# Keeping the FFN's transposed input in DRAM between the two halves of an attention and FFN kernel

## The reference, cut to what matters

```
xn  = layernorm(x, eps=1e-5)
attention:
  xm  = xn * time_mix + shift_by_one_token(xn) * (1 - time_mix)
  k   = exp(min(xm @ Wk.T, 60));  v = xm @ Wv.T;  r = xm @ Wr.T
  wkv, sum_k = decayed sums over earlier tokens of k * v and of k (16 heads, T = 1024)
  a   = (sigmoid(r) * wkv / (sum_k + 1e-16)) @ Wo.T
ffn:
  xf    = layernorm(xn, eps=1e-3) * ln_gamma + ln_beta
  gamma = max |xf| over ALL tokens and channels;  beta = mean |weight|
  w_q   = clip(round(weight / (beta + 1e-5)), -1, 1)
  xq    = clip(xf * 128 / gamma, -128 + 1e-5, 128 - 1e-5)
  f     = (xq @ w_q) * (gamma * beta / 128)
out = x + a + f
```

## Time and profile before

| | |
|---|---|
| runs | 988.46, 988.88, 989.01 us; median 988.88 |
| profiled execution | span 987.2 us, first to last instruction; its own time is not given apart from the span |
| instructions | 14552 |
| DMA | 72.81 MB, 36520 packets on SP's queue, 20.9% of 16 engines |
| chain that ended last | PE 41%, DVE 28%, issue 14%, ACT 10%, DMA 4%, POOL 2% |

### The profile page before, as it was taken

How to read it: one execution, slowest core, us unless ns; L and a number is a source line. 1 busy time by engine, 2 the same in 40 slices (tenths; PEclk the granted TensorE clock), 3 DMA queues, 4 the chain that set the end, 5 groups by cost and what they waited for, 6 DMA issues and landing times.

```text
span 987.2 us, 14552 instructions
## 1 busy us (share of the span) xinstructions
PE 936.3 (95%) x4418; PEld 757.4 (77%) x4418; DVE 806.9 (82%) x1418; ACT 549.3 (56%) x881; POOL 278.9 (28%) x428
## 2 busy tenths in 40 slices
PE   5589999999999999997999999999999999999998
PEld 4478778777877787775787877887878778788786
DVE  5788988889888989895788787797888787878875
ACT  5365756666665757474554454646555546556432
POOL 4332424152415232432303314024023050230300
PEclk9889999999999999999999999999999999999999
DMA  8010302030302121213104113131131221320302
GB/s 317 24 43 25 104 31 97 0 127 0 111 17 86 41 85 42 85 42 128 37 34 144 43 44 129 42 128 63 64 129 42 85 85 42 106 72 36 129 1 85
DMA packets 36560, 72.81 MB, mean 74 GB/s; under 512 B 1180, under 2 KB 1192, under 8 KB 36520
## 3 DMA queue, kind: packets, MB, share of 16 engines
q1 hardware_dynamic: 36520, 72.36, 20.9%
HBM read 47.19 MB, written 25.17 MB: 73 GB/s over the span
## 4 chain that ended last, share of the span: by engine, by line
PE 41%; DVE 28%; issue 14%; ACT 10%; DMA 4%; POOL 2%; DVEq 0%; ACTq 0%; SPq 0%; POOLq 0%
PE kvr L403 7%; PE kvr L405 7%; PE kvr L404 7%; DVE scans L802 7%; PE out_banks L436 5%; PE out_banks L438 5%; PE transposed L342 4%; DVE bn_stats L677 3%; PE out_banks L418 3%; PE out_banks L420 2%; PE out_banks L419 2%; DVE rwkv_lo L822 2%; DVE k_and_kv L792 2%; DVE k_and_kv L818 2%; DVE evacuated L725 2%
## 5 line engine op out<-in xcount | busy, mean ns | idle before, releaser
L968 POOL TENSOR_SCALAR normed<-x,own_stats 128x512 f32<-128x512 f32 x68 | 88.7, 1312 | 239.2 <-PE transposed L342 231.9
L948 POOL TENSOR_SCALAR stat_work<-mean_var 128x4 f32<-128x4 f32 x32 | 10.9, 339 | 344.8 <-DVE mean_var L682 319.8
L403 PE MATMUL kvr<-xm_hi,wv_hi 128*128 128x512 f32 x256 | 107.4, 419 | 0.0
L403 PE MATMUL kvr<-xm_hi,wk_hi 128*128 128x512 f32 x256 | 106.5, 416 | 0.0
L403 PE MATMUL kvr<-xm_hi,wr_hi 128*128 128x512 f32 x256 | 105.8, 413 | 0.0
L418 PE MATMUL out_banks<-wo_hi,rwkv_hi 128*128 128x512 f32 x256 | 103.0, 402 | 2.4 <-DVE rwkv_lo L822 2.4
L405 PE MATMUL kvr<-xm_hi,wv_lo 128*128 128x512 f32 x256 | 101.7, 397 | 0.0
L420 PE MATMUL out_banks<-wo_hi,rwkv_lo 128*128 128x512 f32 x256 | 101.2, 395 | 0.0
L419 PE MATMUL out_banks<-wo_lo,rwkv_hi 128*128 128x512 f32 x256 | 101.2, 395 | 0.0
L436 PE MATMUL out_banks<-w_ternary,ffn_hi 128*128 128x512 f32 x256 | 100.4, 392 | 0.7 <-DVE ffn_lo L749 0.5
L404 PE MATMUL kvr<-xm_lo,wv_hi 128*128 128x512 f32 x256 | 100.9, 394 | 0.0
(11 more groups left out here) (126 smaller groups left out, 2151.3 us busy)
## 6 DMA issues: line engine op xcount, KB each, us to landing
x<-in_L_attn_x SPq DMA_DIRECT2D x16, 1024.0 KB, 5.3
other<-in_L_attn_x SPq DMA_DIRECT2D x16, 1024.0 KB, 5.3
attn_scratch<-x SPq DMA_DIRECT2D x8, 1024.0 KB, 4.3
parked<-attn_scratch SPq DMA_DIRECT2D x8, 1024.0 KB, 6.7
out<-parked SPq DMA_DIRECT2D x8, 1024.0 KB, 4.3
out<-x SPq DMA_DIRECT2D x7, 1024.0 KB, 4.4
parked<-in_L_attn_Wk SPq DMA_DIRECT2D x1, 1024.0 KB, 7.9
other<-in_L_attn_Wv SPq DMA_DIRECT2D x1, 1024.0 KB, 10.1
```

What stands on the lines that cost most here:

```text
L403: nc.tensor.matmul(KVR[:, m, :], hi, XH[t][:, ch, :], start=(ch == 0), stop=False)
L968: last = G.tensor_scalar(dst[:, q, :], src[:, q, :], stats[:, 2 * ffn, q:q + 1], stats[:, 2 * ffn + 1, q:q + 1], ALU.mult, ALU.add)
```

## The change

- Half A stores each FFN slot as it is evacuated (gamma and beta applied, before any scaling) to a DRAM tensor `ffn_input`, 256 KB a slot, 16 slots a batch, from `U`, which becomes a ring of four. ACT waits for the store of a buffer before it writes it again.
- Half B has no FFN transposes, no statistics and no normalisation of "other", and none of own tiles for the FFN. SP loads each chunk into ZA, once ACT has read the chunk of the tile before; ACT copies it from ZA into `U`, scaled by 128 / gamma in the same instruction. Clip, split, low part and ffn_out stay as they are. PE's slots of kinds ffn_* are left out.
- At the seam, the first tile of B is loaded from DRAM within the last batch of A. The reduction of the maximum and POOL's all-reduce are moved into that batch (DVE at group 21), the four scalar operations before the adds of attn1, and the ternary weights are made in four pieces in groups 13 to 16. `gamma_scaled` and `beta_scaled` are gone.
- SP's program is written out batch by batch, with the stores and loads between its old issues.

The diff, cut to its core:

```
-        U = sb("evacuated", [P, 2, TILE])
+        U = sb("evacuated", [P, RING, TILE])
...
-        RING = 2
+RING = 4
...
+    ffn_in = nc.dram_tensor("ffn_input", (B, 2, CH, P, TILE), F32, kind="Internal").ap()
...
+            def store_ffn_input(b, n):
+                kind, ch = SLOTS[n]
+                bb = b + HALF if "other" in kind else b
+                sp.wait_ge(act_u, slots_before(b, "A", n) + 1)
+                sp.dma_start(ffn_in[bb, int(kind[-1]), ch], U[:, n % RING, :]).then_inc(s_fst[n % RING], 16)
+
+            def batch_a(b, is_last=False):
+                for n in range(7):
+                    store_ffn_input(b, n)
+                sp.wait_ge(pe_t, slots_before(b, "A", first_slot("ffn_other0") + CH))
+                sp.dma_start(ZA[:, :, :], x_t[b + HALF, 1]).then_inc(s_oth, 16)
+                store_ffn_input(b, 7)
+                store_ffn_input(b, 12)
+                sp.wait_ge(dve_out, BANKS + bank_use(b, "A", "attn0") + Q)
+                sp.dma_start(scratch_t[b, 0], X[0][:, :, :]).then_inc(s_xst[0], 16)
+                store_ffn_input(b, 13)
+                sp.wait_ge(s_xst[0], 16 * b + 16)
+                sp.dma_start(X[0][:, :, :], x_t[b + 1, 0]).then_inc(s_x[0], 16)
+                for n in range(14, 19):
+                    store_ffn_input(b, n)
...
+                if is_last:
+                    for r in range(RING):
+                        sp.wait_ge(s_fst[r], 16 * CH * HALF)
+                    sp.wait_ge(pe_t, slots_before(b, "A", first_slot("ffn_other1") + CH))
+                    for ch in range(CH):
+                        sp.dma_start(ZA[:, ch, :], ffn_in[HALF, 0, ch]).then_inc(s_fld[ch], 16)
...
+            def load_ffn_input(b, what, ch):
+                bb = b - HALF if "other" in what else b
+                if what == "own0":
+                    sp.wait_ge(act_u, slots_before(b - 1, "B", first_slot("ffn_other1") + ch) + 1)
+                else:
+                    last = FFN_TILES[FFN_TILES.index(what) - 1]
+                    sp.wait_ge(act_u, slots_before(b, "B", first_slot(f"ffn_{last}") + ch) + 1)
+                sp.dma_start(ZA[:, ch, :], ffn_in[bb, int(what[-1]), ch]).then_inc(s_fld[ch], 16)
+
+            def batch_b(b, is_last=False):
+                for ch in range(CH):
+                    load_ffn_input(b, "other0", ch)
+                for ch in range(CH):
+                    load_ffn_input(b, "own1", ch)
+                sp.wait_ge(dve_out, BANKS + bank_use(b, "B", "other0") + Q)
+                sp.dma_start(out_t[b - HALF, 0], ZB[:, :, :]).then_inc(s_parkst, 16)
+                load_ffn_input(b, "other1", 0)
...
             def batch(b, ph, is_last=False):
                 for g in range(GROUPS):
                     n = slot_ahead(g, is_last)
+                    if n is not None and ph == "B" and not SLOTS[n][0].startswith("mix"):
+                        n = None
...
-                act.wait_ge(pe_t, m + 1)
-                act.wait_ge(dve_lo, m + 1)
-                r = n % 2
+                mix = kind.startswith("mix")
+                if mix or ph != "B":
+                    act.wait_ge(pe_t, transposed_before(b, ph, n) + 1)
+                act.wait_ge(dve_lo, m + (RING - 1 if mix else 1))
+                r = n % RING
+                if ph == "A":
+                    act.wait_ge(s_fst[r], 16 * ffn_stores_before(b, n))
...
-                    nc.scalar.activation(U[:, r, :], bank, ACT.Identity, bias=betq[:, ch:ch + 1],
-                                         scale=gamq[:, ch:ch + 1]).then_inc(act_u, 1)
+                    act.wait_ge(s_fld[ch], 16 * (CH * (b - HALF) + FFN_TILES.index(kind[4:]) + 1))
+                    nc.scalar.activation(U[:, r, :], ZA[:, ch, :], ACT.Copy,
+                                         scale=sc[:, 4:5]).then_inc(act_u, 1)
...
+                    if last_a and g in TERNARY_AT:
+                        i = TERNARY_AT[g]
+                        act.wait_ge(dve_q, 3)
+                        nc.scalar.activation(WQ[:, i, :], ZB[:, i, :], ACT.Sign,
+                                             bias=round_c[:, :]).then_inc(act_q, 1)
...
+                    if last_a and g == 21:
+                        gamma()
...
-                if not is_last:
-                    tile_stats(b + 1, "other0", is_last)
+                if ph == "A" and not last_a:
+                    tile_stats(b + 1, ph, "other0", is_last)
+                    largest(b)
+                if last_a:
+                    scales()
                 add_out(b, ph, "attn1")
...
+            def batch_b(b, is_last=False):
+                mix_scale(*mix_call(b, "B", "own1"), own[:, 1])
+                pool.wait_ge(pe_t, transposed_before(b, "B", first_slot("mix_own1")))
+                normalise(XN, X[1], own[:, 1], 0, pool_xn)
+                if not is_last:
+                    mix_scale(*mix_call(b, "B", "next0"), own[:, 0])
+                    pool.wait_ge(pe_t, transposed_before(b, "B", first_slot("mix_own1") + CH))
+                    normalise(XN, X[0], own[:, 0], 0, pool_xn)
```

More of the change, by code:

```diff
@@ L49 @@
 FFN_AFTER = {4: "own0", 8: "other0", 16: "own1", 20: "other1"}
+FFN_TILES = ["own0", "other0", "own1", "other1"]
+RING = 4
 BANK_USES = {"A": ["attn0", "attn1"],
@@ L222, in first_slot, with normed_count, last_normed, stats_number @@
             return SLOTS.index((kind, 0))
[L224 to L231, removed]
+        def normed_count(b, ph, kind):
+            if ph == "A":
+                return 4 * b + [k for k in SLOT_KINDS if "other" not in k].index(kind) + 1
+            return 4 * HALF + 2 * (b - HALF) + ["mix_own1", "mix_next0"].index(kind) + 1
+        def last_normed(b, ph, t):
+            if ph == "A":
+                return normed_count(b, ph, f"ffn_own{t}")
+            return normed_count(b, ph, "mix_own1") - (1 - t)
+        def stats_number(b, ph, tile):
+            if ph == "A":
+                return 4 * b + STATS_ORDER.index(tile) + 1
+            return 4 * HALF + 2 * (b - HALF) + ["own1", "next0"].index(tile) + 1
+        def stats_place(ph, tile):
+            return stats_number(0 if ph == "A" else HALF, ph, tile) % 2
+        def steps_before(i, ph):
+            return STEPS * i if ph == "A" else STEPS * 4 * HALF + MIX_STEPS * (i - 4 * HALF)
         def bank_use(b, ph, what):
@@ L319, in batch @@
                     sp.dma_start(X[1][:, :, :], x_t[b + 1, 1]).then_inc(s_x[1], 16)
-            with sp.Fori(0, HALF) as b:
-                batch(b, "A")
-            sp.wait_ge(act_q, 1)
+            for b in range(HALF - 1):
+                batch_a(b)
+            batch_a(HALF - 1, is_last=True)
+            sp.wait_ge(act_q, CH)
             sp.dma_start(ZB[:, :, :], scratch_t[0, 0]).then_inc(s_park, 16)
-            with sp.Fori(HALF, B - 1) as b:
-                batch(b, "B")
-            batch(B - 1, "B", is_last=True)
+            for b in range(HALF, B - 1):
+                batch_b(b)
+            batch_b(B - 1, is_last=True)
         @block.tensor
@@ L374, in slot @@
             def slot(b, ph, n):
-                kind, _ = slot_of(ph, n)
-                pe.wait_ge(act_u, slots_before(b, ph, n))
+                kind, ch = slot_of(ph, n)
+                if ph == "B" and ch == 0:
+                    pe.wait_ge(act_u, slots_before(b, ph, n - 2 * CH))
+                else:
+                    pe.wait_ge(act_u, slots_before(b, ph, n))
                 if n % CH == 0:
@@ L642, in batch @@
                 rwkv_hi(b, ph, CHUNKS - 1)
-                if not is_last:
-                    normalise(b + 1, "ffn_own0")
-            with act.Fori(0, HALF) as b:
+                if ph == "A" and not last_a:
+                    normalise(b + 1, ph, "ffn_own0")
+            TERNARY_AT = {13: 0, 14: 1, 15: 2, 16: 3}
+            with act.Fori(0, HALF - 1) as b:
                 batch(b, "A")
-            act.wait_ge(dve_q, 3)
-            nc.scalar.activation(WQ[:, :, :], ZB[:, :, :], ACT.Sign, bias=round_c[:, :]).then_inc(act_q, 1)
+            batch(HALF - 1, "A", last_a=True)
             act.wait_ge(dve_s, 5)
```

212 lines of the change are left out of this document (115 added, 97 removed).

## The result

The changed kernel takes 951.31 us (median of 4 runs, 950.51 to 954.09) against 988.81 us (988.46 to 989.01) before: a ratio of 0.9629, 95% interval 0.9614 to 0.9643. The forecast was 950.5.

The account below looks back on a forecast made before the run. PE was taken as the bound, with DVE's chain to the low parts limiting the gain: 987.2 - 30.0 - 8.2 = 949.0 us span, plus 1.7 for the median, 950.5; 945 to 955 at chance 0.55, wider range 942 to 961.

Parts of the forecast that it names:

- The bound: Second-half batches: PE, busy 129.8 of 132.4 us, could give 9.1 us; late FFN low parts limit the gain to 7.5.
- The quarters: Second-half batch: quarters gain 3.7, 0.1 and 3.7 us, the tail 0; 7.5 a batch, 30.0 for four.
- the 0.3 us for a shorter copy: First quarter of a second-half batch: copying out of SBUF shortens the chain to the low part by 0.3 us.
- The seam: First second-half batch: its 9.1 us excess goes, less 0.4 for DVE scalar operations and 0.5 for Sign pieces; net 8.2.
- POOL's 7.1 us lie under attn_out: Seam: gamma's reduce starts over 10 us ahead of its user, so attn_out hides POOL's 7.1 us.
- Statistics and normalisation: Second half: DVE loses 5.8 us a batch, covered by attn_out; POOL and ACT lose work beside PE; priced at nothing.
- Stores: First half: 16 more 256 KB stores a batch cost 0, bounded by 1 us in three batches.
- Loads: Second half: FFN chunk loads cost 0, tightest for other0 at batch start; other end 3 us in each of three batches.
- rival C: Second half: loads of other0 come late behind x1 and ZB, costing 3 us in three batches; 959 to 960 us, chance 0.10.
- The signs named: Steady second-half batches near 125 us, first no longer, clock 1.00; first-half 102.1; ffn_lo waits about 1 us; ACT's DMA wait under 1.
- A: Second half: PE alone sets the time, DVE's chain gives way; 944 us, or 941 without rwkv_lo waits; chance 0.17.
- B: Second half: DVE is the true bound, a batch gives back only DVE's lost 5.8 us; 957.5 us, chance 0.13.

Follow-up runs that it names:

- transposes_back: Changed kernel with four unread identity transposes put back on PE at each FFN slot of the second half: 969.20 us, 0.9799 of the kernel before.
- pool_norm: Changed kernel with ACT's share of the second half's attention normalisation (2 of 4 pieces) moved to POOL: 946.72 us, 0.9573 of the kernel before.
- after_again: The changed kernel unaltered, run again five times for the spread: 951.65 us, 0.9627 of the kernel before, span 949.8.
- stats_back: Changed kernel with two tiles' statistics a second-half batch put back on DVE, on data nothing needs: 957.68 us, 0.9698 of the kernel before.
- late_gamma: Changed kernel with gamma's reduce and scalar operations put back behind the last first-half batch: 951.62 us, 0.9611 of the kernel before.
- double_stores: Changed kernel with each of the 64 stores made twice, ACT waiting for both: 952.16 us, 0.9626 of the kernel before.
- pool_touch: Changed kernel with a small memset on POOL right behind gamma's all-reduce: 951.90 us, 0.9624 of the kernel before.
- no_clip: Changed kernel without the second half's clamp of the FFN input, which acts only on values at the maximum: 946.91 us, 0.9578 of the kernel before.
- early_gamma: Kernel before the change with only gamma's reduction moved into the last first-half batch, no transfer through DRAM: 979.66 us, 0.9902 of the kernel before.
- touch_load_norm: Changed kernel with POOL's memset behind the all-reduce, earlier loads of other0 and all second-half normalisation on POOL: 946.79 us, 0.9576 of the kernel before.
- touch_load_norm_noclip: Changed kernel with POOL's memset, earlier other0 loads, all second-half normalisation on POOL, and no clamp: 941.42 us, 0.9519 of the kernel before.

## Why the forecast was right, step by step

**The bound.** Right: PE sets the pace and the low part of the last FFN chunk takes back part of what it gives. PE lost 7.3 us of busy time between transposes_back and the changed kernel (129.05 to 121.72), and the batch 4.6. With the waits and statistics that went as well it is 7.49 us a batch; 7.5 was forecast. What makes the low part late is ACT's queue as well as DVE's (pool_norm).

**The quarters.** The sum was better than its terms. From the table, before against after: 3.42, 0.86, 2.68 and 0.53 us. The transposes of slots 0 and 13 (0.36 us by attn0 and attn1) lie across those borders, so by slots it is 3.8, 0.5, 3.0 and 0.2, against 3.7, 0.1, 3.7 and 0. The first was right to 0.1, by following one chain through DVE and ACT. The third, which I took to be "built like the first", wasn't: PE's wait there is 1.6 us in place of 1.1. The second was undervalued. The errors (0.1 and 0.4 too little, 0.7 too much, 0.2 too little) cancel, which is luck. One term of the first quarter was too large by itself, the 0.3 us for a shorter copy: the copy takes 0.71 us in the changed kernel and took 0.77.

**The seam.** Mis-sized: 8.2 us forecast, 6.8 measured in after_again (first batch 126.78, 1.9 longer than a steady one, where it was 9.0 longer; and 0.34 us in the last first-half batch, 102.55 against 102.21). In the first profile it is 6.2 (2.5 and 0.3). The step that failed is "POOL's 7.1 us lie under attn_out": they lie ahead of POOL's next tensor_scalar, wherever that is. The 0.9 us charged to the last first-half batch were 0.34. In after_again the first batch has 1.0 us of PE waiting for POOL at the transposes and 0.7 more waiting for ffn_lo than a steady one; no run took POOL's delay away, so that it causes all of the 1.9 us is argued from these waits. In the first profile the clock fell as well (below).

**Statistics and normalisation.** "Priced at nothing" holds for DVE's time, not for all: stats_back gives 2.6 us in the profile and 6 in the medians, mostly since DVE's adds hand the buffers to the transfers.

**Stores.** Right, 0; not even twice the stores cost more than 0.2 us a batch.

**Loads.** Nearly right: no wait in two batches, 0.16 us in the first, and 1.45 in the last; in after_again the last batch has 1.21. In late_gamma, double_stores and pool_touch, whose second half has the same program, the last batch has none and takes 123.8 us, where it takes 125.2 and 124.9 in the two profiles of the changed kernel. So the price is 0 in some executions and 1.1 to 1.4 us in others; "under 1 us" was too little for these. The mechanism of rival C is there, at its threshold: any step that brings the evacuation forward (no_clip) or x1 back (stats_back) makes it wait in more batches.

**The sum.** Span 949.0 forecast; 952.3 and 949.8 in the two profiles. Of after_again's 37.4 us less than before, 1.4 lie ahead of the second first-half batch (it starts at 141.48 in place of 142.91), in the start of the program and its first batch; over the changed kernel and its variants that batch started between 141.2 and 143.1, so I don't count it for the change. The part that the change made in this execution is 36.0 us; forecast, 38.2. Of the 2.2 us between them 1.4 are the seam's and 0.6 the last batch's, which gave 6.9 us (131.8 to 124.9) in place of 7.5. That the median came within 0.8 us of the forecast is in part luck: the shortfall of 2.2 us is about what the start of the program varies by from one execution to the next.

**The signs named.** Steady batches of 124.9 us, first-half batches of 102.1, the waits for ffn_lo twice a batch (1.1 and 1.6 us) and DVE at 81% came as named. A first batch of the second half no longer than the others, at a clock of 1.00, did not (127.4 us at 0.99), nor did a wait of ACT for DMA under 1 us (1.6).

**The rivals.** A: out as an end, by transposes_back (17.5 us against its 28), and since 11 us of waits for ffn_lo stand in the trace; a steady batch falls by 0.85 us without the clamp, by 2.2 with the normalisation off ACT, by 2.95 with both and early loads. B: out by stats_back and by transposes_back. The Trainium skill (Perfetto Trace Analysis, Identifying the Most-Contended Engine) compares weight loads with the other engines' occupancy. By that DVE comes first in the steady batch of this kernel too (100.83 against 98.92 us), yet 2.9 us of DVE work put back twice a batch cost only a part of itself (0.3 to 1.6 us a batch, and part of that by a transfer), and 7.0 us of PE work put back cost 4.6. The nearer guide here was PE's matmul time, 129.05 of 129.50 us in transposes_back.

## What to carry to other kernels

Take work off the engine that is busy throughout, then follow one chain through the other engines to the point where they hand their result back: the smaller of the two gains is the gain, and a quarter that looks the same needs its own walk. Before claiming that a delay is now covered, ask what the delay belongs to; here it moved to the next instruction of a kind. When a transfer's slack is about a microsecond, each later improvement of the consumer will spend it, so move its issue first.

## What was not expected of the hardware

POOL's first tensor_scalar behind a partition all-reduce started late in every kernel here. Where its input came long after the reduce, it started 6.9 to 7.6 us after that input (6.9 in the changed kernel and in late_gamma, 7.3 in pool_touch, 7.6 in no_clip); where its input was there already, it started 7.08 us (before) and 8.4 us (early_gamma) after the reduce. A memset right behind the reduce started at once.

A single short wait of PE was followed, in two executions, by a fall of the clock. Here is the first of the two (first batch of the second half, changed kernel). Until the wait PE had issued a matmul each 0.23 us without a gap:

```profile
489.70 0.50 PE L519 MATMUL out_banks<-w_ternary,ffn_hi 128*128 128x512 f32 x1 [1.78 <-DVE ffn_lo L850]
490.04 0.40 PE L521 MATMUL out_banks<-w_ternary,ffn_lo 128*128 128x512 f32 x1
...
491.29 0.63 PE L519 MATMUL out_banks<-w_ternary,ffn_hi 128*128 128x512 f32 x1
491.72 0.63 PE L521 MATMUL out_banks<-w_ternary,ffn_lo 128*128 128x512 f32 x1
...
493.85 0.63 PE L488 MATMUL kvr<-xm_hi,wk_lo 128*128 128x512 f32 x1
494.28 0.49 PE L486 MATMUL kvr<-xm_hi,wk_hi 128*128 128x512 f32 x1
```

Matmuls of 0.63 us, the lower level of 1.2 GHz, last from 491.3 to 494.3. Against after_again the ffn_out and the projections behind it are 0.85 and 0.70 us longer (10.53 and 12.67 against 9.68 and 11.97), some 1.5 us for the fall. There the same wait is 1.76 us, after one of 1.0 us for POOL at the transposes, and no matmul behind it is slow; nor is one behind the 2.08 us wait of the last batch. The second execution is late_gamma's: again a wait of 1.78 us at this matmul, matmuls of 0.63 us from 489.4 to 491.1, and an ffn_out of 11.16 us against 9.68. Behind the waits of 3.6 us for POOL in pool_norm and touch_load_norm the matmuls are slow too, behind the 1.96 us in touch_load_norm_noclip and waits of up to 2.17 us in stats_back they are not. What decided it stays open. It is part of the difference between the two profiles of one kernel.
